# Cross attention: query tiles evicted whole, score operand assembled by transfers inside SBUF

## What is computed

```
x = x + cross_attention(layernorm(x), ctx, ctx, mask)
# cross_attention, 16 heads of 16 channels:
Q = split_heads(query @ Wq.T + bq); K = split_heads(key @ Wk.T + bk); V = split_heads(value @ Wv.T + bv)
scores = einsum('bhqd,bhkd->bhqk', Q, K) / sqrt(16)
scores = where(mask == 0, -1e10, scores)
h = einsum('bhqk,bhkd->bhqd', softmax(scores), V)
return merge_heads(h) @ Wo.T + bo
```

## Time and profile before

| | |
|---|---|
| median of 3 runs | 762.86 us (761.26 to 763.99) |
| the profiled execution | 768.46 us, its span 766.7 us |
| PE busy | 596.7 us, 78% |
| DVE busy | 527.2 us, 69% |
| ACT busy | 321.1 us, 42% |
| POOL busy | 334.6 us, 44% |
| cross attention, from the first instruction to the next block's first load | 168.2 us |

### The profile page before, as it was taken

How to read it: one execution, slowest core, us unless ns; L and a number is a source line. 1 busy time by engine, 2 the same in 40 slices (tenths; PEclk the granted TensorE clock), 3 DMA queues, 4 the chain that set the end, 5 groups by cost and what they waited for, 6 DMA issues and landing times. The chain is left out here.

```text
span 766.7 us, 12626 instructions
## 1 busy us (share of the span) xinstructions
PE 596.7 (78%) x3566; PEld 494.8 (65%) x3567; DVE 527.2 (69%) x996; ACT 321.1 (42%) x593; POOL 334.6 (44%) x296
## 2 busy tenths in 40 slices
PE   5488888963488998999999977678105989987995
PEld 4477877952356777777777766367004878866874
DVE  5898888957229888888888877475702566567563
ACT  2244555412158778778778760323101121211120
POOL 4343434436015444444445432045370295797145
PEclk9789999995599999999999999775555999999998
DMA  6000000000210000000000000843325034043000
GB/s 204 1 0 1 2 0 1 1 8 0 83 31 1 1 2 1 2 0 0 0 0 0 0 1 0 315 147 144 144 104 181 15 138 176 7 158 156 21 14 4
DMA packets 18480, 39.57 MB, mean 52 GB/s; under 512 B 2362, under 2 KB 13627, under 8 KB 16394
## 3 DMA queue, kind: packets, MB, share of 16 engines
q1 hardware_dynamic: 14570, 32.86, 12.2%
q0 software_dynamic: 1776, 4.23, 1.5%
q10 hardware_dynamic: 2096, 2.05, 0.8%
HBM read 31.58 MB, written 8.21 MB: 52 GB/s over the span
## 5 line engine op out<-in xcount | busy, mean ns | idle before, releaser
L881 POOL TENSOR_SCALAR h_p<-h_p,h_rs 128x1024 f32<-128x1024 f32 x64 | 72.2, 1129 | 122.4 <-DVE h_rs L999 119.9
L1008 DVE TENSOR_REDUCE h_nmx<-h_psS 128x1 f32<-128x1024 f32 x64 | 78.0, 1219 | 21.0 <-PE h_psS L1095 20.3
L949 ACT ACTIVATE h_p<-h_psS,h_nmx 128x1024 f32<-128x1024 f32 x64 | 71.7, 1120 | 28.4 <-DVE h_nmx L1008 28.0
L986 DVE TENSOR_TENSOR h_pTl<-h_psT,h_pTh 128x512 fp32r<-128x512 f32 x128 | 81.2, 675 | 2.1 <-ACT h_pTh L924 2.1
L1058 PE MATMUL h_psT<-ident,h_p 128*128 128x128 f32 x512 | 71.6, 277 | 12.5 <-DVE h_pTl L986 12.3
L1058 PEld LDWEIGHTS h_psT<-ident,h_p 128*128 128x128 f32 x512 | 57.2, 140 | 30.9 <-DVE h_pTl L986 17.8
L298 POOL TENSOR_TENSOR a_p<-a_p,a_rs 128x616 f32<-128x616 f32 x32 | 39.0, 1220 | 78.7 <-DVE a_rs L347 78.7
L924 ACT CAST h_pTh<-h_psT 128x512 fp32r<-128x512 f32 x128 | 69.8, 590 | 7.5 <-PE h_psT L1058 6.7
L1069 PE MATMUL h_psO<-h_pTh,h_vs 128*128 128x256 f32 x256 | 68.0, 301 | 4.0 <-DVE h_oT L993 3.6
L1069 PE MATMUL h_psO<-h_pTl,h_vs 128*128 128x256 f32 x256 | 62.1, 279 | 0.0
L1545 ACT CAST e_xh<-e_psX 128x256 fp32r<-128x256 f32 x22 | 8.2, 374 | 124.4 <-PE e_psX L1616 124.4
(11 more groups left out here) (269 smaller groups left out, 1541.0 us busy)
## 6 DMA issues: line engine op xcount, KB each, us to landing
wst<-in_m_w SPq DMA_DIRECT2D x16, 1024.0 KB, 6.1
bias<-in_m_b SPq DMA_DIRECT2D x8, 640.0 KB, 8.2
rows<-c_blank SPq DMA_DIRECT2D x1, 3250.0 KB, 18.8
xg<-rows SPq DMA_DIRECT2D x1, 2990.0 KB, 11.4
x_all<-in_x SPq DMA_DIRECT2D x2, 768.0 KB, 10.8
whead<-in_f_w ACTq DMA_DIRECT2D x4, 192.0 KB, 3.6
whead<-in_f_w SPq DMA_DIRECT2D x4, 192.0 KB, 4.4
a_wk<-in_xa_wk ACTq DMA_DIRECT2D x1, 512.0 KB, 4.1
```

Of the source, the lines that this page charges most:

```text
L881: pool.tensor_scalar(pr[:, c % 4], pr[:, c % 4], rs[:, c:c + 1], 0.0, ALU.mult, ALU.add).then_inc(pn_ready, 1)
L949: act.activation(pr[:, c % 4], psS[c % 2][:], ACT.Exp, bias=nmx[:, c:c + 1], scale=1.0, accum_out=sm[:, c:c + 1]).then_inc(exp_done, 1)
L986: vec.tensor_tensor(pTl[c // QP % 2][part], psT[hf][:], pTh[c // QP % 2][part], ALU.subtract).then_inc(pT_lo, 1)
L1008: vec.tensor_reduce(nmx[:, c:c + 1], psS[c % 2][:], AX.X, ALU.max, negate=True).then_inc(max_ready, 1)
```

## The change

A step's Q is evicted in whole 128x256 tiles: ACT writes two instructions into a new tile `qhi`, DVE two into a new tile `qlo`, both without crossing partitions. SP then waits for `q_lo` and issues four transfers inside SBUF, each of 64 partitions by 2048 bytes (128 KB), that build `qs` from them: two of them keep their partitions, two cross to the other half. PE's wait ahead of the first scores of a step is now for `q_in`, the count of landed transfers; its wait ahead of `values` stays at `q_lo`. ACT has a new wait ahead of `query_high`, for the transfers of the step before (they read `qhi`). SP waits, from step 2 on, for the scores of two steps back to be done, since they read the `qs` that it overwrites.

```
+        qhi, qlo = sb("a_qhi", [P, KD, W], F32R), sb("a_qlo", [P, KD, W], F32R)
+        MOVES = 4 * 16
...
+            low_half, high_half = slice(0, HP), slice(HP, P)
+            for n in range(NT):
+                to = qs[n % 2]
+                sp.wait_ge(q_lo, n + 1)
+                if n >= 2:
+                    sp.wait_ge(s_ps, U * (n - 1))
+                sp.dma_start(to[low_half, 0].bitcast(F32), qhi[low_half].bitcast(F32)).then_inc(q_in, 16)
+                sp.dma_start(to[high_half, 1].bitcast(F32), qhi[high_half].bitcast(F32)).then_inc(q_in, 16)
+                sp.dma_start(to[high_half, 0].bitcast(F32), qlo[low_half].bitcast(F32)).then_inc(q_in, 16)
+                sp.dma_start(to[low_half, 1].bitcast(F32), qlo[high_half].bitcast(F32)).then_inc(q_in, 16)
...
             def query_high(i, n):
                 upto(act, q_ps, i, 2, n + 1)
-                for a in range(2):
-                    for m in range(KD):
-                        half = slice(a * HP, (a + 1) * HP)
-                        ins = act.activation(qs[n % 2][half, a, m], psQ[half, m], ACT.Identity,
-                                             bias=bq[half, m:m + 1], scale=1.0)
+                upto(act, q_in, i, 2 * MOVES, MOVES * n)
+                for m in range(KD):
+                    ins = act.activation(qhi[:, m], psQ[:, m], ACT.Identity, bias=bq[:, m:m + 1], scale=1.0)
                 ins.then_inc(q_hi, 1)
...
             def query_low(i, n):
                 upto(vec, q_hi, i, 2, n + 1)
-                for a in range(2):
-                    for m in range(KD):
-                        half, other = slice(a * HP, (a + 1) * HP), slice((1 - a) * HP, (2 - a) * HP)
-                        ins = vec.scalar_tensor_tensor(qs[n % 2][other, a, m], psQ[half, m], bq[half, m:m + 1],
-                                                       qs[n % 2][half, a, m], ALU.add, ALU.subtract)
+                for m in range(KD):
+                    ins = vec.scalar_tensor_tensor(qlo[:, m], psQ[:, m], bq[:, m:m + 1], qhi[:, m],
+                                                   ALU.add, ALU.subtract)
                 ins.then_inc(q_lo, 1)
...
                     if u == 0:
-                        upto(pe, q_lo, i, 2, c + 1)
+                        upto(pe, q_in, i, 2 * MOVES, MOVES * (c + 1))
```

More of the change, by code:

```diff
@@ L125, in cross_attention @@
                  "ident_s", "consts", "keep_s", "k_ps", "k_sb", "klT_s", "kh_s", "kl_s", "v_ps", "v_s", "vrep_ps",
-                 "vblk_s", "xT_ps", "x_read", "q_ps", "q_hi", "q_lo", "s_ps", "sub_done", "exp_done", "rs_s", "pn_s",
+                 "vblk_s", "xT_ps", "x_read", "q_ps", "q_hi", "q_lo", "q_in", "s_ps", "sub_done", "exp_done", "rs_s", "pn_s",
                  "pT_ps", "pT_sb", "h_ps", "h_sb", "o_ps")
@@ L129, in cross_attention @@
          ident_ready, consts, keep_ready, k_ps, k_sb, klT_ready, kh_ready, kl_ready, v_ps, v_ready, vrep_ps,
-         vblk_ready, xT_ps, x_read, q_ps, q_hi, q_lo, s_ps, sub_done, exp_done, rs_ready, pn_ready,
+         vblk_ready, xT_ps, x_read, q_ps, q_hi, q_lo, q_in, s_ps, sub_done, exp_done, rs_ready, pn_ready,
          pT_ps, pT_sb, h_ps, h_sb, o_ps) = (sem("a_" + n) for n in names)
```

## The result

| | before | after |
|---|---|---|
| median of the first series, 4 runs each | 763.42 us | 755.18 us (754.67 to 755.70) |
| ratio after to before | | 0.9895, 95% interval 0.9872 to 0.9918 |
| profiled execution, its span | 766.7 us | 753.6 us |
| attention, to the next block's first load | 168.22 us | 162.87 us |
| the rest of that profile | 598.5 us | 590.7 us |

Two later series gave ratios of 0.9924 (0.9896 to 0.9951) and 0.9908 (0.9879 to 0.9937). Over all series the medians are 762.93 us before (76 runs) and 756.46 us after (22 runs), 6.5 us apart. The last two series put the kernel at 757.37 us, inside the range, and at 756.45 us, on its lower edge. So two questions stand: why the attention gained 5.35 us and not 3.7, and where the rest comes from.

A forecast was written before the change was run, and what follows sets the result against it. Attention steps were taken as bound by a cycle of DVE (12.7 us) and PE (3.8 us); −5.3 us on DVE and +1.6 at the start made −3.7, 764.8 against the profile, 759.2 us as median, range 756.5 to 764.0.

The forecast's parts named there:

- the saving on DVE: Evictions in `query_low`: two instructions fewer at 0.445 us each, 0.89 us per step, counted six times, −5.3 us.
- the start: Step 0: transfers not hidden, PE starts the first scores late, +1.6 us, bounds +0.5 and +4.7.
- the cover: Loop steps: 8.2 us from the end of `query_low` to PE's wait, against 4.0 us for transfers to land.
- D: Rival, chance 0.10: transfers land behind the cover every step, PE waits for `q_in` ahead of u = 0 scores; about 780.
- the clock: PE in step 0: lower level may last through projection and next scores, up to 2.7 us more; counted as nothing.
- The larger estimate of +2.3: Step 0 stall by the skill's figures: four transfers need 2 + 2.5 us behind the wake, instead of +1.6.
- I carry the difference over: Conversion from profile to median: 764.8 us lowered by the 5.6 us (0.7%) between profiled execution and median, giving 759.2.
- B: Rival, chance 0.15: start costs much more, +4.4 to +4.7 against −5.3; 762 to 763 us, no change.
- C: Rival, chance 0.10: loop gives back half through a wait on DVE or ahead of u = 0 scores; about 761.8.
- E: Rival, chance 0.03: evictions not shortened, 128 partitions take twice as long; +2.5, 765.4 us.
- the unseen: Remaining chance of 0.02 for what the prediction does not see, counted under slower.
- A: The forecast itself, chance 0.60: 757.6 to 760.8 us, −5.3 with a stall of 0.5 to about 3.

The follow-up runs named there:

- act_four: Changed kernel, but ACT evicts in four instructions of 64x256 into the new tile: median 758.16 us, ratio 0.9942 (0.9920 to 0.9964).
- no_transfers: Kernel before with whole 128x256 evictions straight into `qs`, no transfers, scores not the reference's: step 15.48 us, attention end 160.76 us, whole time 756.28 us, not compared.
- moves_late: Changed kernel, but SP holds each step's transfers, except the first, until DVE's subtractions of the step before are done: 785.79 us, ratio 1.0309.

## Why the prediction was wrong

**The term that failed was the saving on DVE: "0.89 us saved each time `query_low` runs", bounded from above by 0.89.** It was 1.28 us. I took the pitch of the old instructions, 0.445 us, for the price of an instruction of 256 columns, and gave it to the new ones. In it were the holds: an instruction alone is 0.39 us, and the switches between the halves of the partitions held four instructions per step for about 0.12 us each, two of them not evictions at all but the sums and the maximum behind. Six times 0.39 more is 2.3 us. With it the steps gave 7.76 and not 5.3 us, of which the start took back 2.54 and not 1.6, and 0.13 came in the tail: 5.35 in the attention against 3.7. That is 1.65 of the 4.5 us by which the first series missed the forecast; the other 2.9 lie behind the attention (below). The upper bound was no bound, as it left out what the evictions do to their neighbours. Rows before the change show it, to one who compares starts: from reciprocal to maximum 0.23 us behind the evictions (119.74, 119.97).

**What was right.** Partitions cost nothing: 482 ns on 64, 474 ns on 128. The cycle of DVE and PE was read rightly: the wait ahead of u = 0 stayed at 1.35 us, PE did not take over, and all that DVE saved in the six steps passed on. Six steps count, and the seventh saving is lost in the PE-bound tail, which kept its 28.4 us. ACT is worth nothing (`act_four`). The transfers are hidden in the loop (`no_transfers`) with the cover as worked out (8.2 us forecast, 8.0 between the end of the evictions at 98.61 and the scores at 106.65), and D's price is real (`moves_late`).

**The start** cost +1.56 at the first maximum against +1.6. That it was so near is in part luck: waking took 0.03 us and not 0.2, an issue 0.63 and not 0.5, which is 0.2 us more in sum, and the evictions ended at 24.54, 0.13 before the forecast. The other 0.98 us up to the second maximum is the clock, counted as nothing, with 2.7 kept for the range. It fell inside that. The mechanism behind it is less sure than the sum made it. The larger estimate of +2.3, from the figures of the Trainium skill, "SBUF — State Buffer", sections "The DMA setup-cost knee" and "Door 1: The DMA port swizzle", was nearly right in its own term: PE started 4.34 us behind SP's first issue, and 2 + 2.5 are 4.5. The trace agrees with its 196 to 218 GB/s for 64 partitions: 205 GB/s in the burst. That the first maximum came only 1.56 us later is also because wake and evictions were shorter than reckoned, and the first scores' matmuls had started at 27.29 before, 0.2 behind the 27.08 from which the +1.6 and the +2.3 were counted.

**The conversion to a median.** The second step that failed is "I carry the difference over", with later stages that simply shift. −5.35 us in the attention would be 757.5 us (762.86 − 5.35), inside the range, and so would be the prediction's sum with the right term on DVE. The first series lay 2.3 us below that, the later ones at 757.37 and 756.45. Over all series 1.4 us of gain lie behind the attention, and their cause stays open. The rest varied from 589.9 to 598.5 us in the profiles, which I had not reckoned with; that is wider than the term that the rest was meant to carry. Of the rivals none came true: B's start was 2.5 and not 4.4 to 4.7, C's waits and D's late landings are not there, and E is refuted by the 474 ns. Two numbers were loose without touching the forecast: D, E and the unseen add up to 0.15 and not 0.13, and A's lower end, 757.6, has no stall in it, where a stall of 0.5 gives 758.1.

## What to carry to other kernels

Read an engine's cost from start to start, over the neighbours too: a group of half-height instructions costs more than its durations, because each change of the start partition, on the way in and on the way back out, holds an instruction, here for about 0.12 us; where it can't be avoided, order the halves so that the last one starts where the next instruction does. Moving data across partitions by transfers inside SBUF is free where a step of slack is there, here 4.2 us of 8, and costs its whole latency the first time. Before a difference is shared out over the stages of one pair of profiles, profile the kernel before again: here one stage that nobody had touched moved by 6 us.

## What was not expected of the hardware

- A DVE instruction that starts on another half of the partitions than the one ahead: 0.11 to 0.13 us, without any wait shown in the rows. The order of four equal instructions was worth 0.3 us (3.47 and 3.77 us).
- Transfers of 128 KB inside SBUF, 64 partitions each, four in a row on one queue, land 2.3 us (2.2 to 2.7) after their issues, 0.63 us apart. Such a burst keeps the DMA engines at a share of 0.93 with 205 GB/s. Issuing two of the four ahead of the evictions, from ACT, saved 1.28 us.
- The clock's return in step 0 came at two places for one and the same kernel, 5.15 and 4.00 us from the first to the second maximum.
- One more fall of the clock some 505 to 525 us behind the attention (0.91 instead of 1.00) stood in three of seventeen profiles, the three with the longest rests, 597.3 to 598.5 us against at most 593.7.
